# Rotary sine products for two sequences at once, and all attention normalisation on GpSimd, in a fused transformer step

## The reference, cut to what matters

```
h = tok(x)
h = h + attn(layernorm(h), Wq, Wk, Wv, Wo)
h = h + ffn(layernorm(h))

attn:  q = rope(x @ Wq), 12 heads of 64;  k = rope(x @ Wk), v = x @ Wv, 3 heads of 64, each for 4 q heads
       rope: concatenate([x1 * c + x2 * s, -x1 * s + x2 * c])
       out = softmax(q k^T * SCALE) v;  out @ Wo
```

## Time and profile before

| what | us |
|---|---|
| median of 3 runs | 993.04 |
| lowest and highest | 992.38, 993.05 |
| span of the profiled execution | 994.2 |
| PE, DVE, ACT, POOL busy in it | 962.1, 815.9, 680.0, 655.9 |

### The profile page before, as it was taken

How to read it: one execution, slowest core, us unless ns; L and a number is a source line. 1 busy time by engine, 2 the same in 40 slices (tenths; PEclk the granted TensorE clock), 3 DMA queues, 4 the chain that set the end, 5 groups by cost and what they waited for, 6 DMA issues and landing times.

```text
span 994.2 us, 25841 instructions
## 1 busy us (share of the span) xinstructions
PE 962.1 (97%) x7402; PEld 831.6 (84%) x7402; DVE 815.9 (82%) x1997; ACT 680.0 (68%) x2469; POOL 655.9 (66%) x936
## 2 busy tenths in 40 slices
PE   7889999999999999999999999999999999999988
PEld 4778888898888898888898888888888888888877
DVE  4788888888888888888888888888888888888862
ACT  3557677667777667777667767666767666867653
POOL 2677666777666767666767666767666677766670
PEclk9999999999999999999999999999999999999999
DMA  6044554444554444545444545444445444445330
GB/s 192 23 128 107 146 145 125 123 126 114 149 141 133 115 132 111 153 135 141 112 134 112 144 135 145 114 132 117 136 135 149 114 131 120 131 135 153 97 108 22
DMA packets 193633, 124.56 MB, mean 125 GB/s; under 512 B 31185, under 2 KB 185169, under 8 KB 193617
## 3 DMA queue, kind: packets, MB, share of 16 engines
q1 hardware_dynamic: 190880, 120.98, 44.3%
q10 hardware_dynamic: 2736, 3.38, 1.0%
HBM read 69.26 MB, written 55.05 MB: 125 GB/s over the span
## 4 chain that ended last, share of the span: by engine, by line
PE 65%; DMA 16%; DVE 6%; SPq 6%; issue 3%; POOL 2%; ACT 1%; DVEq 0%; POOLq 0%
PE ring L846 14%; PE ring L1061 13%; PE ring L917 8%; DMA ET<-spill 8%; DMA spill<-EB 8%; PE ring L824 6%; SPq L253 5%; PE ring L884 5%; PE bank L865 5%; PE ring L985 3%; DVE EB L596 2%; PE ring L994 2%; PE bank L994 2%; PE bank L1028 2%; PE ring L981 1%
## 5 line engine op out<-in xcount | busy, mean ns | idle before, releaser
L330 ACT ACTIVATE E<-ring,m_neg 128x128 f32<-128x128 f32 x768 | 273.2, 380 | 19.2 <-DVE m_neg L582 18.2
L468 POOL TENSOR_TENSOR qkT<-rot_c,rot_s 128x256 f32<-128x256 f32 x256 | 187.3, 732 | 20.1
L476 POOL TENSOR_TENSOR E<-E,e_rcp 128x512 f32<-128x512 f32 x158 | 175.2, 1124 | 37.0 <-DVE e_rcp L605 37.0
L330 ACT ACTIVATION_READ_ACCUMULATOR E<-ring,m_neg 128x1 f32 x768 | 166.8, 217 | 0.0
L466 POOL TENSOR_TENSOR rot_s<-rot_s,rope_qs 128x256 f32<-128x256 f32 x192 | 146.5, 763 | 2.8 <-DVE rot_s L570 2.4
L865 PE MATMUL bank<-wout_sb,G 128*128 128x192 f32 x744 | 141.1, 326 | 0.0
L582 DVE TENSOR_REDUCE m_neg<-ring 128x4 f32<-128x512 f32 x192 | 129.9, 678 | 9.8 <-PE ring L884 9.8
L596 DVE STREAM_TRANSPOSE EB<-E 128x512 f32<-128x512 f32 x186 | 124.9, 687 | 15.1 <-POOL E L476 15.1
L1061 PE MATMUL ring<-wo_sb,OT 128*128 128x192 f32 x744 | 133.5, 329 | 0.5 <-DVE OT L627 0.4
L1061 PEld LDWEIGHTS ring<-wo_sb,OT 128*128 128x128 f32 x744 | 119.4, 190 | 7.4 <-issue 7.4
L865 PEld LDWEIGHTS bank<-wout_sb,G 128*128 128x128 f32 x744 | 119.7, 190 | 0.4 <-issue 0.4
(11 more groups left out here) (159 smaller groups left out, 2486.3 us busy)
## 6 DMA issues: line engine op xcount, KB each, us to landing
spill<-EB SPq DMA_DIRECT2D x186, 256.0 KB, 2.3
ET<-spill SPq DMA_DIRECT2D x248, 128.0 KB, 2.8
ET<-spill SPq DMA_DIRECT2D x248, 64.0 KB, 2.3
x_sb<-in_x_dram SPq DMA_DIRECT2D x64, 192.0 KB, 2.5
out_dram<-out_sb SPq DMA_DIRECT2D x62, 96.0 KB, 2.3
x_sb<-in_x_dram SPq DMA_DIRECT2D x64, 64.0 KB, 2.4
w_raw<-in_w_att_dram ACTq DMA_DIRECT2D x2, 608.0 KB, 5.0
win_raw<-in_w_in_dram ACTq DMA_DIRECT2D x2, 384.0 KB, 6.3
```

The lines of the kernel that those rows point to most:

```text
L330: last = nc.scalar.activation(E[:, a, s * P:(s + 1) * P], RING[a][:, s * P:(s + 1) * P], ACT.Exp, bias=m_neg[:, a, s:s + 1], accum_out=e_s ...
L468: nc.gpsimd.tensor_tensor(qkT[:, b, :, a], rot_c[:, b, :, a], rot_s[:, b, :, a], ALU.add).then_inc(q_out, 1)
L476: nc.gpsimd.tensor_tensor(e, e, r, ALU.mult).then_inc(prob_out, 1)
```

## The change

Three edits, and semaphore counts that follow from them.

- GpSimd's rotation: the sine product is done once for a tile, for both sequences (512 columns), followed by the sum of sequence 0 (256 columns), for the four tiles; then the sums of sequence 1 follow, two tiles in one instruction (512 columns), tiles 2 and 3 first, then 0 and 1. That is 10 instructions in place of 16. scores(0) waits for the four first sums, as before.
- All three banks of sequence 0 are normalised on GpSimd (6 `probs` a step in place of 5); VectorE's `normalised` is left out except in step 0.
- On VectorE sums_inverted(0, 0) moves ahead of key_max(0, 2), and the second bank of heads_out behind it.

```diff
-                def rotated(a, i, done):
+                def rotated_first(i):
                     b = PROJ[i]
                     pool.wait_ge(rot_out, 4 * p + i + 1)
-                    sin = (rope_ks if b == 3 else rope_qs)[:].rearrange("p (o t) -> p o t", o=1).broadcast_to([P, 2, P])
-                    nc.gpsimd.tensor_tensor(rot_s[:, b, :, a], rot_s[:, b, :, a], sin, ALU.mult).then_inc(sin_out, 1)
-                    pool.wait_ge(sin_out, 8 * p + done)
-                    nc.gpsimd.tensor_tensor(qkT[:, b, :, a], rot_c[:, b, :, a], rot_s[:, b, :, a],
+                    sin = (rope_ks if b == 3 else rope_qs)[:].rearrange("p (o t) -> p o t", o=1).broadcast_to([P, 4, P])
+                    both = rot_s[:, b].rearrange("p c a t -> p (c a) t")
+                    nc.gpsimd.tensor_tensor(both, both, sin, ALU.mult).then_inc(sin_out, 1)
+                    pool.wait_ge(sin_out, 4 * p + i + 1)
+                    nc.gpsimd.tensor_tensor(qkT[:, b, :, 0], rot_c[:, b, :, 0], rot_s[:, b, :, 0],
+                                            ALU.add).then_inc(q_out, 1)
+
+                def rotated_second(b):
+                    nc.gpsimd.tensor_tensor(qkT[:, b:b + 2, :, 1], rot_c[:, b:b + 2, :, 1], rot_s[:, b:b + 2, :, 1],
                                             ALU.add).then_inc(q_out, 1)
...
                     for i in range(4):
-                        rotated(0, i, i + 1)
-                    for i in range(4):
-                        rotated(1, i, i + 5)
+                        rotated_first(i)
+                    rotated_second(2)
+                    rotated_second(0)
                 if att and not (isinstance(p, int) and p == 0):
-                    probs(0, 1, p)
-                    probs(0, 2, p)
+                    for k in range(NKV):
+                        probs(0, k, p)
...
                 if ffn and att:
-                    heads_out(p - 1)
-                if att:
+                    heads_out(p - 1, (0,))
+                if att:
+                    sums_inverted(0, 0, p)
                     key_max(0, (2,))
-                    sums_inverted(0, 0, p)
+                if ffn and att:
+                    heads_out(p - 1, (1,))
...
                 elif att:
                     sums_inverted(0, 1, p)
-                    normalised(0, p)
...
-                    pe.wait_ge(q_out, 8 * p + 4 * a + 4)
+                    pe.wait_ge(q_out, 6 * p + 2 * a + 4)
```

More of the change, by code:

```diff
@@ L563, in rotate @@
                     if i == 0:
-                        need(dve, q_out, 8 * p)
+                        need(dve, q_out, 6 * p)
                     dve.wait_ge(qk_mm, 4 * p + i + 1)
@@ L590, in blocks_turned @@
                     h0 = REP * g - s0
[L591 to L594, removed]
+                    dve.wait_ge(prob_out, 6 * q + 3 * a + k - 2)
                     need(dve, spilled[k], 16 * (2 * (q - 1) + a + 1))
@@ L621, in last_copied, with heads_out @@
                         LAST_T[k].rearrange("p (h i c) -> p h i c", h=REP, i=NB)).then_inc(last_out, 1)
-                def heads_out(q, ring=RING[1]):
-                    for b, c in enumerate((slice(0, 512), slice(512, DQ))):
+                def heads_out(q, banks=(0, 1), ring=RING[1]):
+                    for b in banks:
+                        c = (slice(0, 512), slice(512, DQ))[b]
                         heads = (c.stop - c.start) // P
@@ L798, in step @@
                         last_copied(k)
-                    heads_out(p, RING[0])
+                    heads_out(p, (0, 1), RING[0])
                 elif att:
@@ L931, in last_probs_turned @@
                     g = GROUPS[k]
-                    pe.wait_ge(prob_out, 5 * p + 3 + k - 2)
+                    pe.wait_ge(prob_out, 6 * p + 3 + k - 2)
                     if k == 2:
```

## The result

The changed kernel takes 1046.43 us (median of 4 runs, 1046.08 to 1047.07) against 993.04 us: slower by a ratio of 1.0533, 95% interval 1.052 to 1.0546. The prediction was 1044.3 us with a range of 1012 to 1062, and slower with a chance of 0.93.

What follows compares the result with a forecast made beforehand. TensorE's instruction list was taken as the bound; wider GpSimd products delay scores(0), 32 x 8.34 - 215.6 = 51.3 us, all other parts 0 or left out, giving 1044.3 us from 993.04, range 1012 to 1062.

Steps and rivals of the forecast that it cites:

- The bound and the slack: TensorE's instruction list is the path; in step 16 the fourth sum is ready 0.60 us before scores(0) starts.
- The wide product: GpSimd's 512-column sine product was taken as 1.29 us, bounded by 1.04 and 1.46 us, against 0.73 us for 256 columns.
- The sum: scores(0) starts 8.34 us after the first product in each of 32 steps, against 215.6 us in total: 51.3 us lost.
- Nothing given back: Everything behind scores(0), including exponentials, blocks and DMA, moves with it; waits at probs_v stay, so no return.
- VectorE's multiplication worth 0: Removing VectorE's 1.11 us multiplication gains 0 us; without the TensorE and ScalarE cover, up to 1.11 us a step.
- GpSimd's third multiplication worth 0: On GpSimd behind the rotation, the third multiplication has its input at the same point as before: 0 us.
- The port: VectorE's t_a and GpSimd instructions hold each other up in SBUF; at most 3 us in all, left out.
- 1: GpSimd's wide product costs only 1.04 us, like the multiplication of E: 19.3 us lost, 1012 us; chance 0.10.
- 2: GpSimd's wide product costs as much as two halves, 1.46 us: 73 us lost, 1066 us; chance 0.07.
- 3: VectorE's freed 1.11 us shortens the wait at probs_v: at most 34 us given back, 1010 us; chance 0.07.
- 4: Not slower: GpSimd's instruction price is mostly fixed and slack swallows the change, 993 or some 990 us; chance 0.07.
- The signs named beforehand: Products about 1.29 us, TensorE idle some 1.5 us before scores, step 31.2 us, DVE about 34 us less busy, probs_v idle unchanged.

Runs made afterwards that it cites:

- e7: The changed kernel with only the last of the four products ahead of scores(0) wide, missing halves done behind: 1015.73 us, ratio 1.0222.
- e4: The changed kernel with only the last two of the four products ahead of scores(0) wide, missing halves done behind: 1022.12 us, ratio 1.0275.
- e1: The kernel before with only the new GpSimd rotation; VectorE keeps its multiplication and order: 1046.84 us, ratio 1.0513.
- e6: The changed kernel with four of TensorE's feed-forward products moved from behind probs_v(1, p-1) to ahead of scores(0): 1042.63 us, ratio 1.0492.
- e5: The kernel before without VectorE's multiplication in steps 1 to 31, one bank of sequence 0 left unnormalised: 993.26 us, ratio 0.9997.
- e12: e11 with GpSimd's first sequence 0 multiplication between the two wide sums and VectorE turning the first block ahead of h: 988.48 us, ratio 0.9952.
- e2: The changed kernel with the old rotation: all sequence 0 multiplications on GpSimd and VectorE's new order alone: 1002.53 us, ratio 1.0068.
- e3: The changed kernel with four narrow products ahead of scores(0); behind them, products of 256 and 768 columns and two 512-column sums: 1020.59 us, ratio 1.0255.
- e8: The kernel before with all eight products narrow and only sequence 1's sums wide, in two 512-column instructions; VectorE keeps its multiplication: 993.39 us, ratio 0.9994.
- e10: e3 with the sums of sequence 1 as four instructions of 256 columns in place of two of 512: 1002.78 us, ratio 1.0098.
- e13: e12 with layer norm hn moved ahead of the third multiplication on GpSimd and the third block on VectorE: 993.76 us, ratio 1.0005 to the kernel before.
- e11: The changed kernel with the rotation of e8, keeping all sequence 0 multiplications on GpSimd and VectorE's new order: 993.22 us, ratio 0.9999.

## Why the prediction was right

- **The bound and the slack.** TensorE's list was the path, and scores(0) had 0.6 us to spare. Right. e7 shows the slack directly: 0.555 us more ahead of scores(0), and TensorE's products wait there in the last step only (2.2 us; its weight loads in 12 steps, 4.5 us in all, against 2.9 us in 2). e4 shows the sum step by step (15.4 us expected, 17.6 after 2.2 measured at that wait).
- **The wide product.** 1.29 us taken, 1.281 and 1.294 us measured. The straight line between instructions of the same kind held; the ends of the range, 1.04 us (a repeated input) and 1.46 us (no saving), were both wrong.
- **The sum.** 51.3 us expected. In the traces the distance from the first product to scores(0), added over the 32 steps, went from 215.6 to 265.7 us, 50.1 more (8.30 us a step where 8.34 was written), and the wait from 2.2 to 50.6 us. The medians differ by 53.4 us. e1 shows that the rotation makes all of it that can be told from noise.
- **Nothing given back.** Right to within 3 us: the wait at probs_v stayed (39.4 us of PEld after 42.3, 5.6 of PE after 8.6). But I reasoned with one chain only, that over the blocks and the DMA. e6 showed a second that is tied to scores(0) and is nearer to binding when TensorE's list gets shorter, the copy to OT; the sentence was right and its reason incomplete.
- **VectorE's multiplication worth 0.** Right, by e5 to within 0.15% (1.5 us). "Up to 1.11 us a step" would have needed something on VectorE to do in that gap; e12 put it there and won 4.7 us of the possible 34.
- **GpSimd's third multiplication worth 0.** Right only beside the new rotation, which ends early against the exponentials. With the old one it costs 8 us (e2). The step that was missing: what stands behind it on GpSimd, the variance for hn, whose wait had little to spare.
- **The port.** I left it out of the sum and allowed 3 us. In the changed kernel t_a takes 0.674 us where it took 0.520, and TensorE's loads wait 12.9 us for it after 12.4: nothing. The position had been worked out (the wide sum to end 2.4 us after scores(0), and it did), but that it was harmless is a matter of 1 us: here t_a comes 0.88 us after the second wide sum has started and has 0.39 us of it left to wait for. In e3 it comes 0.16 us after the first has started, and the waits for t_a and OT grow by 24.5 of the 26 us lost. In e7 they grow by 19.5 of 22.5 us. In e4, where most of the loss is the scores' own wait, they grow by 8.4 of 27.6 us. I missed it in all three expectations although the trace of before had shown it (t_a and a product holding each other up). The Trainium skill, SBUF — State Buffer, section SBUF: two separate sides, states that a VectorE instruction with two SBUF inputs and a GpSimd one exclude each other for the whole instruction. The traces of e3, e7, e8 and e10 agree for t_a: a median of 1.354 us behind a wide sum (e3), 0.425 us when it is first (e8).
- **Rivals.** 1 and 2 fell with the duration, 3 with e5, 4 with the 32 waits. The signs named beforehand came true: a step takes 31.3 us (t_a turned at 535.37 and 566.70) where 31.2 was written, and DVE is busy 32.5 us less (34 written).

That the medians differ by 53.4 us and the profiled spans by 49.8 us has to do with the profile of before. A run's device time is some 2 to 3 us more than its core's span (1046.08 and 1044.0 us here; other runs of the kernel before with 993.0 to 993.3 us have spans of 990.0 to 991.5 us). Its profiled span of 994.2 us belongs to an execution some 3 us slower than the median, and the 1.2 us given ahead of the prediction compare a span with a device time. So the trace accounts for 48.4 us in the waits for the sums, and some 5 us of the 53.4 are not found in them.

Left open: those 5 us, and where the last 1.5 us of e3's loss went: it is 26 us, and the waits for t_a and OT grew by 18.3 and 6.2 us. I didn't try a t_a that reads a single SBUF tensor.

## What to carry to other kernels

Merging two instructions into one saves its fixed part (here 2 x 0.73 us became 1.28) but delivers the first half later; before merging, ask who waits for the first half and how much slack there is, in the step's timeline and not in the busy shares: GpSimd was 66% busy and 0.6 us from the path. Do the narrow work that someone waits for first, and merge behind it. And relief for an engine that waits right afterwards is worth nothing until some work is moved into the gap.

Before lengthening a GpSimd instruction, look at what VectorE starts while it runs: the operation with two SBUF inputs (t_a) stood behind it for all that was left of it, and the tensor_scalar from SBUF to SBUF (hn, e13) took 1.09 us in place of 0.38.

## What the runs showed of the hardware

- A GpSimd product or sum of two full float32 inputs takes 0.731 us for 256 columns, 1.27 to 1.29 for 512 and 1.815 for 768 (e3): some 0.19 us and 2.1 ns a column. With one input that repeats a single column over 128 it is 1.041 us for 512 (L481), a fifth less for the same output.
- VectorE's t_a (256 columns, two SBUF inputs) takes 0.425 us when it is first (e11), 0.84 us when it meets a narrow GpSimd instruction (e10) and a median of 1.354 us behind a wide one (e3). Behind a GpSimd instruction it ends 0.28 us after that one's end, and 0.01 us in who starts first decides between 0.43 and 1.54 us (e7). A maximum over the scores in PSUM (L604 in e3, L587) stays at 0.65 to 0.69 us in all 192 cases, beside the same GpSimd instructions.
- The granted clock stayed at 1.00, the level of 2.4 GHz, through the middle of the changed kernel (90 to 980 us), with TensorE idle for some 1.6 us in every step.
